# Sampled attention: exponential ahead of the copies, values copied in the order in which they are summed, interpolation shares kept as pairs, and the products of the values on VectorE

## The reference, cut to what matters

```python
loc_x = jnp.mod(ref + off + loc, sign_lens[:, None, None, None])
xg = loc_x / (key_len - 1) * 2.0 - 1.0
ix = ((xg + 1.0) * key_len - 1.0) / 2.0
x0 = jnp.floor(ix)
dx = ix - x0
...
w0 = (1.0 - dx)[..., None]
w1 = dx[..., None]
sk = 0.5 * (w0 * _gather_pad0(Kh, i0) + w1 * _gather_pad0(Kh, i1))
sv = 0.5 * (w0 * _gather_pad0(Vh, i0) + w1 * _gather_pad0(Vh, i1))
scores = jnp.einsum('bhqd,bhqkd->bhqk', Qh / math.sqrt(HD), sk)
attn = jax.nn.softmax(scores, axis=-1)
ctx = jnp.einsum('bhqk,bhqkd->bhqd', attn, sv)
```

## Time and profile before

| | us |
|---|---|
| median of 3 runs (2138.39 to 2145.12) | 2143.85 |
| the profiled execution | 2157.57 |
| its span | 2155.8 |
| from the first to the last instruction of the sampled-attention units, in the trace | 843.93 to 1142.12 |
| DVE busy, whole span | 1036.9 (48%) |
| PE busy, whole span | 1257.2 (58%) |
| POOL busy, whole span | 599.7 (28%) |

### The profile page before, as it was taken

The page is one execution under the profiler, slowest core; times in us unless marked ns, Lnnn a source line. Parts: engine busy times, 40 slices in busy tenths (PEclk is TensorE's granted clock), DMA queues, the critical chain, the costliest instruction groups (busy, mean ns, idle before and its releaser), DMA issues. The chain is left out here.

```text
span 2155.8 us, 26038 instructions
## 1 busy us (share of the span) xinstructions
PE 1257.2 (58%) x9140; PEld 769.6 (36%) x9140; DVE 1036.9 (48%) x2829; ACT 516.8 (24%) x1036; POOL 599.7 (28%) x716
## 2 busy tenths in 40 slices
PE   1478887788659714435342295389727917883120
PEld 1233333334348703434342285123226802321000
DVE  2454454546313227786876164343232224426696
ACT  0123332333214302112120131133304402331000
POOL 5132222211150052232212502400050061005675
PEclk9978888989779955555555598588858958985555
DMA  5900000000211114323310124000011110001332
GB/s 159 398 25 0 1 1 0 1 1 1 81 42 57 60 34 122 77 65 85 96 46 4 50 65 141 21 0 1 0 32 60 62 39 0 1 0 58 93 103 78
DMA packets 73252, 116.45 MB, mean 54 GB/s; under 512 B 11565, under 2 KB 52320, under 8 KB 70624
## 3 DMA queue, kind: packets, MB, share of 16 engines
q1 hardware_dynamic: 60320, 85.24, 13.2%
q0 software_dynamic: 12800, 29.51, 4.8%
HBM read 77.03 MB, written 37.68 MB: 53 GB/s over the span
## 5 line engine op out<-in xcount | busy, mean ns | idle before, releaser
L1453 POOL DMA_INDIRECT arena<-ys_d,slot_i x96 | 91.3, 951 | 339.5 <-DMA ys_d<-arena 311.2
L1101 DVE CUSTOM_DVE_ANT_0 arena<-ps,far 128x512 f32<-128x512 f32 (+3 forms) x256 | 118.3, 489 | 104.8 <-PE ps L794 103.4
L2223 POOL DMA_INDIRECT arena<-in_w_ud,arena x128 | 130.7, 1021 | 50.9 <-issue 37.8
L2573 PE MATMUL ps<-wide,arena 78*128 78x32 bf16 x3840 | 109.3, 188 | 58.5 <-ACT wide L2675 50.5
L718 POOL TENSOR_SCALAR_AFFINE_SELECT arena<-arena 128x260 f32<-128x260 f32 (+1 forms) x128 | 53.2, 428 | 320.2 <-ACT arena L973 320.2
L2573 PEld LDWEIGHTS ps<-wide,arena 78*128 78x128 bf16 x3840 | 108.7, 104 | 63.6 <-ACT wide L2675 51.4
L1712 PEld LDWEIGHTS ps<-arena 128*128 128x128 f32 (+1 forms) x1012 | 123.4, 192 | 4.0
L1712 PE MATMUL ps<-arena 128*128 128x128 f32 (+1 forms) x1012 | 123.6, 275 | 0.0
L1444 POOL DMA_INDIRECT xs_d<-arena,slot_i x96 | 93.9, 978 | 92.9 <-DVE slot_i L1519 64.6
L816 PE MATMUL ps<-arena 32*128 32x128 f32 (+3 forms) x512 | 116.4, 501 | 1.1 <-DVE arena L1120 1.1
L973 ACT ACTIVATE arena<-ps 128x1024 f32<-128x1024 f32 (+1 forms) x96 | 84.8, 883 | 110.7 <-PE ps L816 110.4
(11 more groups left out here) (463 smaller groups left out, 2682.3 us busy)
## 6 DMA issues: line engine op xcount, KB each, us to landing
arena<-low_d SPq DMA_DIRECT2D x32, 780.0 KB
xs_d<-zrow SPq DMA_DIRECT2D x1, 10240.0 KB, 30.4
ys_d<-zrow SPq DMA_DIRECT2D x1, 10240.0 KB, 56.2
arena<-xs_d SPq DMA_DIRECT2D x69, 128.0 KB, 2.0
ys_d<-arena SPq DMA_DIRECT2D x69, 128.0 KB, 1.7
arena<-in_w SPq DMA_DIRECT2D x2, 1408.0 KB, 8.5
wide<-in_Wfc SPq DMA_DIRECT2D x1, 2048.0 KB, 11.8
wide<-in_Wproj SPq DMA_DIRECT2D x8, 256.0 KB, 6.7
```

Source lines behind the costliest of these rows:

```text
L1101: ins = nc.vector.tensor_tensor_reduce(junk[:, n % 2, 384 * i:384 * i + w], ps[:, n % 2, 384 * i:384 * i + w], far[:, T - w:T], 1.0, 3 * N ...
L1453: pool.indirect_dma_start(out=yg[:, t % 4, j, :], out_offset=None, in_=ys_d, in_offset=bass.IndirectOffsetOnAxis(ap=slot_i[:, j, t:t + 1], ...
L2223: pool.indirect_dma_start(out=rows_g[:, t % 4, h, :], out_offset=None, in_=A["w_ud"], in_offset=bass.IndirectOffsetOnAxis(ap=eidi[:, t % 4 ...
L2573: mm = nc.tensor.matmul(ps[:, 2 * (i % 3) + h // 2, col:col + 4 * HD], ring[m_ % 4][:, h * NK + p_, t % 2 * P:t % 2 * P + P], table[n // 4 ...
```

## The change

On ACT the exponential of unit n - 1 stands ahead of all copies of unit n. The values are copied so that the 10 numbers that one output sums (5 points, 2 neighbours) lie side by side; the tables are laid out for this, and a copy of values now writes pairs. `frac` becomes `share`, which holds (1 - dx, dx) side by side: the interpolation of the scores becomes one product of 160 and one sum over 2, the weights one product of 160; after the positions one more operation of 320 makes 1 - dx. The product of values and weights moves from POOL to DVE, and `outputs` is done in the same unit. At the start, POOL computes the first `rstd` before the four bias operations instead of behind them. Several small tiles are placed in tiles that are otherwise unused in this stage (`picked`, `hot`, `glog`, `bs0`).

```diff
@@ -2344,11 +2344,15 @@
...
-            raw = carve(2, NT, H * NK); frac = carve(2, NT, H * NK)
+            raw = carve(2, NT, H * NK); share = carve(2, NT, H * NK, 2)
...
-            s2 = carve(4 * HG * NK, 2); sd = carve(NT, HG * NK); se = carve(2, NT, HG * NK); sw = carve(2, NT * HG * NK, 2)
-            mx = carve(NT * HG); sums = carve(2, NT * HG); inv = carve(NT * HG); got = carve(NT * HG, HD)
+            s2 = picked[:, :, :, :].rearrange("p a b c -> p (a b c)")[:, 0:2 * NT * POINTS].rearrange("p (t r s) -> p t r s", t=NT, s=2)
+            sw = carve(2, NT, POINTS, 2); mx = carve(NT * HG); inv = carve(NT * HG)
+            se = hot[:, 0, :, :].rearrange("p a b -> p (a b)"), hot[:, 1, :, :].rearrange("p a b -> p (a b)")
+            se = [v[:, 0:NT * POINTS].rearrange("p (t r) -> p t r", t=NT) for v in se]
+            sums = [glog[:, 0:2, :].rearrange("p a b -> p (a b)"), glog[:, 2:4, :].rearrange("p a b -> p (a b)")]
+            got = bs0[:, :]
...
@@ -2365,7 +2369,8 @@
...
-            as_table = lambda v: v.rearrange("j (h s e) -> j h s e", h=H, s=4)
+            keys_of = lambda v: v.rearrange("j (h c) -> j h c", h=H)[:, :, 0:2 * HD].rearrange("j h (s e) -> j h s e", s=2)
+            values_of = lambda v: v.rearrange("j (h c) -> j h c", h=H)[:, :, 2 * HD:4 * HD].rearrange("j h (e s) -> j h s e", s=2)
...
-                o3, j0, dx = raw[:, b % 2, :, :], low[:, b % 2, :, :], frac[:, b % 2, :, :]
+                o3, j0, dx = raw[:, b % 2, :, :], low[:, b % 2, :, :], share[:, b % 2, :, :, 1]
...
                 eng.tensor_tensor(dx, o3, j0, ALU.subtract).then_inc(s1["fix"], 1)
+                eng.wait_ge(s1["fix"], b + 1)
+                ch.link(eng.tensor_scalar(share[:, b % 2, :, :, 0], dx, -1.0, 1.0, ALU.mult, ALU.add))
...
-                    def value_products(n):
-                        pool.wait_ge(s1["w"], n + 1)
-                        v = gv[n % 2].rearrange("p (r e) -> p r e", e=HD)
-                        nc.gpsimd.tensor_tensor(v, v, sw[:, n % 2, :, :].rearrange("p r s -> p (r s)").unsqueeze(2)
-                                                .to_broadcast([P, 2 * NT * POINTS, HD]), ALU.mult).then_inc(s1["vw"], 1)
-
...
-                    bt = as_table(bias_table)
-                    for s, (row_, v) in enumerate(((bk1, 0), (bk1, 1), (bv1, 0), (bv1, 1))):
-                        ins = nc.gpsimd.tensor_scalar(bt[:, :, s, :], row_[0:S2 + 1, :].rearrange("j (h e) -> j h e", h=H),
+                    rstd_of(0)
+                    for part, row_, v in ((keys_of, bk1, 0), (keys_of, bk1, 1), (values_of, bv1, 0), (values_of, bv1, 1)):
+                        ins = nc.gpsimd.tensor_scalar(part(bias_table)[:, :, v, :], row_[0:S2 + 1, :].rearrange("j (h e) -> j h e", h=H),
                                                       in_range[0:S2 + 1, v:v + 1], 0.5, ALU.mult, ALU.mult)
                         ch.link(ins)
-                    rstd_of(0)
...
-                        value_products(n)
...
-                                dst = as_table(raw_table)[:, :, v:4:2, :]
-                                ins = nc.scalar.activation(dst.rearrange("j h s e -> j s h e"), src[:, v, :, :, :], ACT.Copy, scale=0.5)
+                                nc.scalar.activation(keys_of(raw_table)[:, :, v, :], src[:, v, 0, :, :], ACT.Copy, scale=0.5)
+                                ins = nc.scalar.activation(values_of(raw_table)[:, :, v, :], src[:, v, 1, :, :], ACT.Copy, scale=0.5)
...
-                        src = ps[:, 2 * (i % 3):2 * (i % 3) + 2, 0:2 * NK * 4 * HD].rearrange("p k (r s e) -> p k r s e", r=2 * NK, s=2)
+                        src = ps[:, 2 * (i % 3):2 * (i % 3) + 2, 0:2 * NK * 4 * HD].rearrange("p k (r c) -> p k r c", c=4 * HD)
                         M = POINTS * 2 * HD
-                        for s, dst in enumerate((gk, gv)):
-                            ins = nc.scalar.copy(dst[n % 2][:, M * t:M * t + M].rearrange("p (k r e) -> p k r e", k=2, r=2 * NK),
-                                                 src[:, :, :, s, :])
+                        nc.scalar.copy(gk[n % 2][:, M * t:M * t + M].rearrange("p (k r e) -> p k r e", k=2, r=2 * NK),
+                                       src[:, :, :, 0:2 * HD])
+                        ins = nc.scalar.copy(gv[n % 2][:, M * t:M * t + M].rearrange("p (k e r s) -> p k r e s", k=2, e=HD, s=2),
+                                             src[:, :, :, 2 * HD:4 * HD].rearrange("p k r (e s) -> p k r e s", s=2))
                         ins.then_inc(s1["out"], 1)
...
@@ -2697,14 +2697,14 @@
                             lower(0)
                     for n in range(N_UNITS):
                         b, g = n // 4, n % 4
+                        if n:
+                            exps(n - 1)
                         for t in range(NT):
                             taken(n, t)
                             if (g, t) == (0, 1) and b + 1 < B:
                                 table_step(b + 1, 0)
                             if t == 1 and g and b + 1 < B:
                                 table_step(b + 1, g)
-                            if t == 1 and n:
-                                exps(n - 1)
...
-                        ch.link(nc.vector.tensor_reduce(s2.rearrange("p r s -> p (r s)"), gk[n % 2].rearrange("p (r e) -> p r e", e=HD),
+                        ch.link(nc.vector.tensor_reduce(s2.rearrange("p t r s -> p (t r s)"), gk[n % 2].rearrange("p (r e) -> p r e", e=HD),
                                                         AX_X, ALU.add))
-                        pair = s2.rearrange("p (t r) s -> p t r s", t=NT)
-                        e_ = se[:, n % 2, :, :]
-                        ch.link(nc.vector.tensor_tensor(sd, pair[:, :, :, 1], pair[:, :, :, 0], ALU.subtract))
-                        ch.link(nc.vector.tensor_tensor(sd, sd, frac[:, b % 2, :, gs_], ALU.mult))
-                        ch.link(nc.vector.tensor_tensor(e_, sd, pair[:, :, :, 0], ALU.add))
+                        e_ = se[n % 2]
+                        ch.link(nc.vector.tensor_tensor(s2, s2, share[:, b % 2, :, gs_, :], ALU.mult))
+                        ch.link(nc.vector.tensor_reduce(e_, s2, AX_X, ALU.add))
...
-                        e_ = se[:, n % 2, :, :]
-                        if n >= 2:
-                            dve.wait_ge(s1["vw"], n - 1)
-                        sw4 = sw[:, n % 2, :, :].rearrange("p (t r) s -> p t r s", t=NT)
-                        ch.link(nc.vector.tensor_tensor(sw4[:, :, :, 1], e_, frac[:, b % 2, :, gs_], ALU.mult))
-                        nc.vector.tensor_tensor(sw4[:, :, :, 0], e_, sw4[:, :, :, 1], ALU.subtract).then_inc(s1["w"], 1)
-                        ch.link(nc.vector.tensor_reduce(sums[:, n % 2, :], e_.rearrange("p t (h k) -> p (t h) k", k=NK), AX_X, ALU.add))
+                        ch.link(nc.vector.tensor_tensor(sw[:, n % 2, :, :, :], share[:, b % 2, :, gs_, :],
+                                                se[n % 2].unsqueeze(3).to_broadcast([P, NT, POINTS, 2]), ALU.mult))
+                        v = gv[n % 2].rearrange("p (k e r) -> p k e r", k=2 * NT, e=HD)
+                        ch.link(nc.vector.tensor_tensor(v, v, sw[:, n % 2, :, :, :].rearrange("p t (k r) s -> p (t k) (r s)", k=2).unsqueeze(2)
+                                                        .to_broadcast([P, 2 * NT, HD, 4 * NK]), ALU.mult))
+                        ch.link(nc.vector.tensor_reduce(sums[n % 2], se[n % 2].rearrange("p t (h k) -> p (t h) k", k=NK), AX_X, ALU.add))
...
-                        ch.link(nc.vector.reciprocal(inv, sums[:, n % 2, :]))
-                        dve.wait_ge(s1["vw"], n + 1)
-                        ch.link(nc.vector.tensor_reduce(got, gv[n % 2].rearrange("p (t r e) -> p t e r", t=NT * HG, r=2 * NK), AX_X, ALU.add))
+                        ch.link(nc.vector.reciprocal(inv, sums[n % 2]))
+                        ch.link(nc.vector.tensor_reduce(got, gv[n % 2].rearrange("p (r x) -> p r x", x=2 * NK), AX_X, ALU.add))
                         if g == 0 and b >= 2:
                             dve.wait_ge(turn7, place["o", b - 2] + 1)
-                        nc.vector.tensor_tensor(o_rows[b % 2][:, :, 32 * g:32 * g + 32].rearrange("p t (h e) -> p t h e", h=HG),
-                                                got.rearrange("p (t h) e -> p t h e", t=NT),
-                                                inv.rearrange("p (t h) -> p t h", t=NT).unsqueeze(3).to_broadcast([P, NT, HG, HD]), ALU.mult)\
+                        nc.vector.tensor_tensor(o_rows[b % 2][:, :, 32 * g:32 * g + 32].rearrange("p t (k h e) -> p t k h e", k=2, h=2),
+                                                got.rearrange("p (t k e h) -> p t k h e", t=NT, k=2, e=HD),
+                                                inv.rearrange("p (t k h) -> p t k h", t=NT, k=2).unsqueeze(4).to_broadcast([P, NT, 2, 2, HD]), ALU.mult)\
                             .then_inc(s1["o"], 1)
...
                         if 2 * n + 4 < 2 * N_UNITS:
```

(6 more changed lines are left out.)

## The result

The changed kernel takes 2075.03 us (median of 4 runs, 2072.30 to 2092.97); the kernel before, with a fourth run beside it, 2144.48 us. The ratio is 0.9687 (95% interval 0.9628 to 0.9747), 54 to 80 us less. Timed again in a later series, the ratio was 0.9724 (0.9690 to 0.9759). Forecast were 2082 us and a range of 2069 to 2100. The profiled execution took 2092.97 us (span 2091.2, against 2155.8 before). In it the stage before ends 7.3 us later and all that follows the units is 6.1 us shorter. None of this was changed, and such shifts stand in every pair of traces here, so the comparison goes by the stage: from the first norm statistics to the first scores (49.9 us before, 47.1 now) and from there to the end of unit 15 (298.2 before, 235.3 now), which I call the stretch. Forecast were 1.5 us off the one and a stretch of 237.4.

A forecast was written before the change was run, and what follows sets the result against it. DVE was taken to bound the sampled attention, with gaps of 63 us. Its terms summed to 237.4 us, 60.8 less than 298.2; with 1.5 at the start, 62.3 off the 2143.85 median gave 2082 us, range 2069 to 2100.

The forecast's parts named there:

- Product on DVE: DVE's product of values and weights takes 1.52 us a unit, between bounds of 1.33 and 2.41.
- Sum of the values: DVE's sum over values now lying side by side falls from 2.46 to 1.52 us a unit.
- Comparisons: With no product on POOL, 14 of DVE's comparisons lose 2.1 us of waiting each, 29.5 us in all.
- Rivals B and C: B: sum keeps 2.42 or product takes 2.41 us, 2096, chance 0.07; C: ring transfers keep comparisons long, 2111, chance 0.03.
- Meetings: POOL's remaining table steps, norms and residuals hold DVE up: 1.5 us taken, bounds 0 and 13.
- Exponential ahead: DVE's 44.1 us of waits for ACT's exponential go, except 0.5 us each in units 14 and 15.
- What is late next: In units 3 and 7 PE's chain makes scores to scores 17.2 us; DVE waits 9.0 twice, 18.1 in all.
- Plain unit: A unit's DVE work without positions or chain takes 11.4 us, against 15.9 before.
- Start: POOL's first rstd ahead of the four bias operations saves 1.5 us before the first comparison.
- Rival A: PE becomes the feed: its unexplained halts exceed the 2.4 us slack, gain falls by 14 us to 2096; chance 0.12.
- Rival D: TensorE's clock rises from 1.2 to 2.4 GHz, saving up to 5 us in each chain: 2072 us; chance 0.10.
- Rival E: Slower than before: ACT's paired value copies take 1.7 us longer or more; at 2.5 us each, 2165; chance 0.02.

The follow-up runs named there:

- the layout run: The changed kernel with the values copied and summed in the old order, operands 8 numbers apart: stretch 248.1 us against 235.3, ratio 0.9724.
- The operations without use: The changed kernel plus one unused POOL operation per unit, in two runs: memset, stretch 235.7 us, ratio 0.9718; addition on 32 partitions, 262.6 us, 0.9810.
- the last version: The changed kernel with TensorE's work for batch b + 2 moved to later places, ACT's copies and DVE's offset reading with it: 2060.98 us, ratio 0.9619.

## Why the prediction was right, and where it was not

- *Bound and gaps*: right. DVE bounds the stretch, and what the stretch gained the program gained.
- *Product on DVE*: 1.49 us (1.52 taken, with the link) and not the 2.41 of the upper bound. Two of the 16 met POOL, the mean is 1.61.
- *Sum of the values*: 1.486, the value taken; the cause is shown by the layout run.
- *Comparisons*: 29.2 us less, 29.5 forecast. That POOL's product and not the transfers stood behind the long ones is shown by the run with the product back on POOL: 2726 against 1659 ns on the mean, with the same transfers. The operations without use show the same shutting out where no data is shared. The rule as the prediction put it names only operations of POOL that read; the comparison was held by a memset too. Rivals B and C are out.
- *Meetings*: two products of the chain's units took 2.44 (+1.9 in all), 1.5 was forecast, near the lower bound as taken. The prediction gave the place in the order as its reason; it was a narrow one. The trace has eight table steps in the stretch, not nine, and six other operations of POOL. All eight steps came 0.45 to 0.63 us after DVE's product had begun, in it and not behind it, and so POOL stood and not DVE. With the exponential behind tile 1 seven of the eight came first, and DVE's busy time grew by 4.1 us. That this term stayed near its lower bound was in part luck.
- *Exponential ahead*: the size was right (0.7 us left, 1.0 forecast), the cause only in half. The step said that the 44.1 us go because the exponential, once ahead, needs only the end of the scores. That is enough by itself: without the early sums 0.7 us are left too, and in the kernel before none. But it is not needed. Put back, it costs 5.5 us, 4.1 of them busy time, and no wait for the exponential outside the chains but the 0.3 us of units 14 and 15. The step mentioned the sums done a unit earlier only as what frees the copies; they free the exponential too, and alone they are worth 36 of the 41.5 us that the two moves give together.
- *What is late next*: right, 17.2 us from scores to scores in the chain; the wait of 8.1 instead of 9.0 is the meeting above. That TensorE's order there is the cause is shown by the last version.
- *Plain unit*: 11.27 us, 11.38 forecast. The stretch came out 2.1 us under the sum.
- *Start*: forecast 1.5 us, measured 2.8, of which the order is 2.4. The term left out the meeting of the normed rows with POOL.
- *Rival A*: TensorE never became the feed. In the changed kernel it stood five times for nothing the profile shows, 7.3 us in all, once 4.1, in round 11; DVE did not wait there. So the slack of 2.4 us with which the rival was reckoned was too small for that round at least.
- *Rival D*: the granted clock did rise in places, to 0.65 on the mean in rounds 3 and 7, but there DVE sets the time: in the run with the late sums the rounds 3 and 7 both take 11.67 us, one with 0.50 and one with 0.65. In the chains, where it would count, it was 0.50 in the first trace; in the second it gave 0.5 us once, far from 10.
- *Rival E*: ACT's copies grew by 0.007 us where E needed 1.7.

In all, 60.8 + 1.5 forecast, 62.9 + 2.8 measured in the traces. The medians moved by 69 us, with an interval of 54 to 80; the stage accounts for 66 of them, and the rest is within that interval.

## What to carry to other kernels

When a wait has two conditions in a row (here copies that wait for sums, and an exponential that stands behind the copies), breaking either one can remove it, as here, and a gain booked to one edit may belong to the other: only the two-by-two tells. An operation that POOL does "for free" may be paid for by DVE, as here, where it lengthened every comparison and every product that it met: look for instructions of one shape that take two durations, and see what stands beside the longer ones. Before moving work between engines, price the busy time that the move frees on the receiving engine, here 31 us against 24.

## What the runs showed of the hardware that was not expected

- The same product on POOL took 2.41 us with its values in the old layout and its weights repeated innermost, and 2.90 in the new one with weights repeated over the middle dimension; DVE did both in 1.49.
- An addition of POOL on only 32 partitions held DVE's product on all 128 for 2.0 us.
- Which operation of POOL meets which of DVE depends on a few tenths: with the exponential behind tile 1 seven table steps came before DVE's operations instead of after them, and the stretch's busy time on DVE grew by 4.1 us without a wait in any list.
- A memset of POOL cost DVE's product nothing (1.49 us), but held up its comparison for 1.0 us where it began first.
